# Moving the two strip-laying transfers from behind the sixth tile's patch requests to behind the last request of a batch

## What is computed

```python
x = x + _L0_conv_ref(_gn(x), W0, b0)
# second block, on h = _gn(x):
offset = conv2d_same(conv2d_same(h, w1, b1), w2, b2)
val = gather(y0, x0) * wy0 * wx0 + gather(y0, x0 + 1) * wy0 * wx1 \
    + gather(y0 + 1, x0) * wy1 * wx0 + gather(y0 + 1, x0 + 1) * wy1 * wx1
x = x + relu(einsum('ogck,bgckhw->bohw', wd, val))
```

## Time and profile before

| what | value |
|---|---|
| median of 3 runs | 460.77 us (460.49 to 461.5) |
| profiled execution, its own time | 459.05 us |
| its span, first to last instruction | 457.0 us |
| mean granted clock of TensorE | 0.97 of full |
| busy: PE, DVE, ACT, POOL | 405.2, 339.5, 215.6, 90.0 us |
| shares of the chain that ended last: PE, DVE, DMA, SP's queue | 46%, 32%, 6%, 5% |

### The profile page before, as it was taken

The page is one execution under the profiler, slowest core; times in us unless marked ns, Lnnn a source line. Parts: engine busy times, 40 slices in busy tenths (PEclk is TensorE's granted clock), DMA queues, the critical chain, the costliest instruction groups (busy, mean ns, idle before and its releaser), DMA issues.

```text
span 457.0 us, 9689 instructions
## 1 busy us (share of the span) xinstructions
PE 405.2 (89%) x3887; PEld 291.9 (64%) x3887; DVE 339.5 (74%) x586; ACT 215.6 (47%) x392; POOL 90.0 (20%) x99
## 2 busy tenths in 40 slices
PE   6698989979998789799999798989869898979996
PEld 6455557646665565678666575768556566857875
DVE  5995776829999999388854999376979945779901
ACT  3343254345555365441655446331845643257661
POOL 5444470001774100000546100000010000000000
PEclk9899999999999899999999899989979997999999
DMA  7200002250011124332001313442213243303330
GB/s 252 77 0 0 0 2 75 84 141 1 2 47 46 47 67 146 85 90 91 12 13 36 92 54 94 124 126 81 59 47 100 90 122 98 104 23 107 96 105 24
DMA packets 46157, 32.71 MB, mean 72 GB/s; under 512 B 3264, under 2 KB 43488, under 8 KB 46112
## 3 DMA queue, kind: packets, MB, share of 16 engines
q1 hardware_dynamic: 46048, 31.95, 23.5%
q10 hardware_dynamic: 64, 0.13, 0.1%
HBM read 25.24 MB, written 10.37 MB: 78 GB/s over the span
## 4 chain that ended last, share of the span: by engine, by line
PE 46%; DVE 32%; DMA 6%; SPq 5%; issue 4%; ACT 4%; POOL 1%; DVEq 0%; ACTq 0%; POOLq 0%
PE psB L788 10%; PE psB L555 9%; PE psT L739 7%; DVE wpix L1507 7%; PE psV L762 5%; DVE combo L1294 4%; PE psA L646 4%; DMA h_scr<-h_ring 3%; SPq L320 3%; DVE combo_p L1298 2%; DVE tent L1488 2%; PE psA L555 2%; DVE tent L1482 2%; PE psB L813 2%; PE psA L813 2%
## 5 line engine op out<-in xcount | busy, mean ns | idle before, releaser
L1021 ACT ACTIVATE wcell<-psT 128x512 f32<-128x512 f32 (+1 forms) x160 | 83.9, 552 | 70.2 <-PE psT L739 68.9
L1507 DVE TENSOR_TENSOR wpix<-tent 128x512 f32<-128x512 f32 (+1 forms) x160 | 99.7, 675 | 14.4 <-PE psT L739 13.3
L739 PE MATMUL psT<-ident,wpix 128*128 128x128 f32 x576 | 89.1, 288 | 12.4 <-ACT wcell L1021 12.0
L739 PEld LDWEIGHTS psT<-ident,wpix 128*128 128x128 f32 x576 | 68.8, 148 | 37.2 <-issue 29.5
L493 POOL TENSOR_TENSOR sim<-rel 128x512 f32<-128x512 f32 x48 | 61.4, 1299 | 69.0 <-ACT rel L978 69.0
L1045 ACT ACTIVATE val<-psV 128x576 f32<-128x576 f32 x64 | 44.0, 688 | 30.7 <-PE psV L762 30.2
L788 PE MATMUL psB<-val,wd_sb 128*128 128x256 f32 x216 | 51.2, 392 | 0.0
L762 PE MATMUL psV<-wcell,hwin 64*32 64x144 f32 x2048 | 47.2, 294 | 3.9 <-ACT val L1045 3.5
L646 PE MATMUL psA<-sim,scratch 128*128 128x512 f32 x96 | 45.6, 597 | 0.6 <-POOL sim L493 0.6
L788 PEld LDWEIGHTS psB<-val,wd_sb 128*128 128x128 f32 x216 | 40.7, 193 | 8.3 <-issue 2.9
L555 PE MATMUL psB<-g_p 128*128 128x512 f32 x144 | 40.9, 419 | 0.0
(11 more groups left out here) (193 smaller groups left out, 453.6 us busy)
## 6 DMA issues: line engine op xcount, KB each, us to landing
hwin<-h_scr SPq DMA_DIRECT2D x128, 128.0 KB, 2.9
h_scr<-h_ring SPq DMA_DIRECT2D x8, 576.0 KB
h_ring<-sim SPq DMA_DIRECT2D x4, 512.0 KB
x_all<-x SPq DMA_DIRECT2D x1, 1536.0 KB, 10.0
out<-yout SPq DMA_DIRECT2D x12, 128.0 KB, 1.8
off_scr<-sim SPq DMA_DIRECT2D x4, 288.0 KB
combo<-sim SPq DMA_DIRECT2D x32, 32.0 KB
val<-w SPq DMA_DIRECT2D x1, 576.0 KB, 6.1
```

Source lines behind the costliest of these rows:

```text
L739: last = pe.transpose(bank[:, at:at + P], wpix[:, t % 2, k, 2 * h:2 * h + 2, :].rearrange("p g q -> p (g q)"), ident[:, :])
L1021: act.activation(wcell[:, t % 2, taps[0]:taps[-1] + 1, :, :].rearrange("q k h p -> q (k h p)"), bank[:, 0:len(taps) * G // 2 * P], ACT.Cop ...
L1507: dve.tensor_tensor(w, ty, tx, ALU.mult).then_inc(s["weights_done"], 1)
```

## The change

`lay_image(b + 1)` no longer stands between the patch requests of tiles 5 and 6 of batch b, but behind those of tile 7, directly ahead of the next batch's first request. The strips of batch 0 are laid as before.

```diff
@@ -411,8 +411,6 @@
                 for t in range(2, ROWT):
                     if t == IMAGE_TILE and b + 1 < B:
                         store_image(b + 1)
-                    if t == IMAGE_TILE + 1 and b + 1 < B:
-                        lay_image(b + 1)
                     if t == ROWT - 1 and b + 1 < B:
                         shift_offsets(b + 1)
                     if t == ROWT - 1 and b == LAST:
@@ -422,6 +420,7 @@
                     for i in range(1, QT):
                         store_tile(i)
                 else:
+                    lay_image(b + 1)
                     for t in range(2):
                         windows(b + 1, t)
                     for m in range(4):
```

## The result

The changed kernel takes **467.35 us**, the median of 6 runs (465.81 to 468.74). The kernel before, run beside it, takes 460.88 (460.09 to 461.5, 6 runs). The ratio is 1.0142 (95% interval 1.0116 to 1.0168), so the change costs **6.5 us**. The profiled execution took 466.67 us with a span of 464.9; before it was 459.05 and 457.0.

The account below looks back on a forecast made before the run. DVE was taken as the bound at batch 1's end, from its last addition on. Terms 4.7 (ahead of batch 2) + 2.8 (batch 3) + 0 (batch 1) + 1.4 (clock) = 8.9 us, on 460.77: 469.7 us, range 465.0 to 474.5.

Parts of the forecast that it names:

- The mechanism: At batch ends, output stores queue behind strips and requests on SP; DVE waits: 4.7 us ahead of batch 2, 2.8 of 3.
- SP's wait for strips: Sign in the changed profile: ahead of the next batch's first request, three more waits of some 12 to 14 us each.
- The first store of batch 1: Sign on SP's queue: issued near 320.6 us instead of 312.48.
- that ahead of batch 1: Boundary ahead of batch 1: store 1.5 us late, but DVE has slack, so 0 us (to 0.6).
- the path from tile 7's requests to the last addition: Batch end: 2.64 + 14.36 + 5.44 + 0.68 + 2.9 us, from tile 7's requests through strips and eight requests to store landing.
- TensorE's clock: Start of batch 3: PE's idle grows to about 4.1 us, the clock falls, costing 1.4 us (0 to 3.3).
- Quick and hidden: Rival: strips land in 5.9 us at their new place, no store is late, 460.8 us; chance 0.05.
- The rule of the Trainium skill's page: Counter-estimate for both strips: about 2.0 us plus bytes over 436 GB/s, 4.7 us, leaving no term of the sum.
- Faster through earlier offset copies: Rival: offset copies land sooner without the strips' tail, gaining 3.7 to 7.1 us; chance 0.04 for a faster kernel.
- Only one boundary pays: Rival: the stall ahead of batch 3 is absorbed and the clock holds, leaving 4.7 us, 465.5 us; chance 0.16.

Follow-up runs that it names:

- E5: Kernel before, with the strips moved at the end of batch 0 alone: 459.85 us, ratio 0.9985.
- E1: Changed kernel, with the stores of the first two quarters issued ahead of the next batch's first patch request: 460.13 us, ratio 0.9997 to the kernel before.
- E2: Changed kernel, with four slots of `yout` in place of two: 460.91 us, ratio 1.001 to the kernel before.
- E3: Kernel before, with four slots of `yout` in place of two, as a control: 459.95 us, ratio 1.0001.
- F2: Changed kernel itself, timed again on another chip: 466.40 us, ratio 1.0126 to the kernel before.
- E7: Kernel before, with the strips moved at the end of batch 2 alone: 463.79 us, ratio 1.0073.
- E9: Changed kernel, with 24 unused identity turns on PE filling its wait ahead of batch 3: 465.95 us, ratio 1.0119 to the kernel before.
- F3: Changed kernel with 24 unused identity turns in PE's wait ahead of batch 3, timed again on another chip: 466.56 us, ratio 1.0130 to the kernel before.
- E4: Changed kernel, with the strip transfers written with 36 rows outermost instead of 4 strips: 460.56 us, ratio 1.0015 to the kernel before.
- E6: Kernel before, with the strips moved at the end of batch 1 alone: 463.05 us, ratio 1.0043.
- F1: Kernel before, without the change, with several of PE's waits filled by 14, 20 or 34 unused identity turns: 455.40 us, ratio 0.9893.

## Why the prediction was right, and where its sizes were off

The time on record was 469.7 us (465.0 to 474.5), slower at 0.91. The measured 467.35 lies inside and the sign is right; the size, 8.9 us, was 2.4 too large.

**The mechanism held, step by step.** SP's wait for strips came three more times (12 to 14 us each were said; from the strips' issue to the first request it is 12.4 to 12.9, of which the view puts a part down to the sampling that SP also waits for, and so shows 40.1 in all for four). The first store of batch 1 went out at 320.84 us, where 320.6 was said. That this is so close is luck: tile 7's requests stood 1.1 us later in this execution, and behind them the store came after 21.6 us, not 22.4. The additions waited for stores at three boundaries, and that ahead of batch 1 cost nothing, in the trace (105.81 us against 105.80) and alone (E5). There PE's releases, for which DVE had waited 1.80 us, took no time any more: behind the late pair DVE runs on into tile 2's `wpix` at 223.63 with no idle time ahead of its pieces. E1 and E2 then showed the cause by taking it away in two ways.

**The term that was mis-sized is the path from tile 7's requests to the last addition,** 26.0 us in the prediction. Measured at the end of batch 1 it is 24.4, from 299.26 to the second addition of the pair at about 323.7 (323.25 + 0.43, and 0.06 more in the chain). Piece by piece:

| piece | predicted | end of batch 1 | end of batch 2 |
|---|---|---|---|
| tile 7's requests | 2.64 | 2.67 | 2.67 |
| strips, first issue to first request | 14.36 | 13.64 | 13.95 |
| eight requests | 5.44 | 5.27 | 5.27 |
| stores, from the first issue | 0.68 + 2.9 | 2.41 + 0.45 | 2.46 + 0.42 |
| sum | 26.0 | 24.4 | 24.8 |

Against the old last addition this leaves 24.4 - (319.51 - 298.16) = 3.1 us where 4.7 was said, and 24.8 - (402.68 - 379.44) = 1.5 where it was 2.8. Three pieces were too long. The step that failed was the store: I let the last addition wait for the second store and gave that a landing of 2.9 us, between the 1.6 and 3.85 of the earlier trace rows. In fact the addition of m = 2 waits for the first store, which lands in 2.4, and by the time that addition is done (0.42 to 0.45 us later) the second, issued 0.68 behind the first, has landed too; that is 0.7 us. Another 0.7 us (0.4 at the end of batch 2) come from the strips: the 14.36 of the one trace I had is the slow end; the changed kernel and the ten later runs that lay them in the same way show 13.5 to 13.9 in batch 0. The eight requests give the last 0.2.

The margins are of one trace too. Against the last additions in E3's trace, where the clock fell otherwise (23.06 and 20.45 us behind tile 7's requests, not 21.35 and 23.24), the same two stores would cost 1.4 and 4.3 us, not 3.1 and 1.5.

**TensorE's clock**, 1.4 us in the sum, was right as an observation: PE's longer wait ahead of batch 3 (2.86 us, about 4 was said) was followed by a lower granted clock, and what follows it, up to the fourth sampling, took 2.3 us more in that trace, and less, 1.0 and 0.9, in F2 and E7. What it is worth in the time stays open (E9, F2, F3).

**The rivals.** "Quick and hidden" fell with the 13.6 to 14.2 us that the strips took; E4 shows that this rival was real but for the transfer's shape: at 7.8 and 9.9 us the loss is gone from the times. The rule of the Trainium skill's page "DMA: Bandwidth & Descriptors", section "Anatomy of one DMA — SWDGE (gpsimd) path", put the two at an estimate of 4.7 us; SP's queue measured three times that, and even with 12 engines 6.7 to 9.9. "Faster through earlier offset copies" fell with the copies' waits, 1.92 and 1.84 us against 1.85. "Only one boundary pays" fell with E6 and E7, which both lose time.

## What to carry to other kernels

A transfer's wait on an in-order queue is paid by whoever depends on what stands behind it there. Before moving a long transfer, list everything issued behind its first waiter and ask which engine needs that for a free buffer; here it was two output stores of 128 KB, not the 1.2 MB of strips that moved. Two remedies brought the time back to that of the kernel before, within 0.3%: issuing those stores first, and giving them slots of their own. A third shortened the wait itself: with 36 rows outermost in place of 4, the busy share of the transfer engines rose from 0.26 to 0.73.

## What the runs showed that I had not expected

- Filling PE's waits with turns whose results nobody uses made the kernel before 4.9 us faster. The waits are short, 1.85 us and 4.33 us, and the clock behind them was 0.72 and 0.50 of full; with the waits filled it was 1.00 in both windows. I had priced such a clock only at the one wait that the change lengthened.
- The same filling in the changed kernel gave a clock of 1.00 and a fourth sampling 1.0 us sooner (12.11 to 11.14) in the trace, but no shorter time.
- The stretch between the copies of batch 0's end and those of batch 1's took 105.8 us in six traces (before, changed, F2, E2, E4, E5) and 107.4 in seven (E1, E3, E6, E7, E9, F1, F3), whatever the edit. What parts them is TensorE's granted clock: over the first six us it was 1.00 in the six and 0.75 to 0.81 in the seven, behind the same wait of 2.7 us for ACT, and the twelve matmuls of `dconv` behind that wait took 2.86 us in the six and 3.68 to 4.30 in the seven. Why the clock falls behind that wait in some executions and not in others, no run here shows. A term of that size is to be read from its own stretch, not from the span.
- Two transfers of 576 KB took 13.5 to 14.9 us with four in the outermost dimension, and 6.7, 6.8, 7.8 and 9.9 us with 36. In the last 4 us of the 9.9 the 16 engines were busy by 0.11 and then 0.05, so one or two of them finished late; why is not shown.
